# Scaling the exponentials of attention by the head gates, with the first loads in another order

## What is computed

```python
Q, K, V = heads(x @ wq.T + bq), heads(x @ wk.T + bk), heads(x @ wv.T + bv)   # 16 heads of 32
scores = jnp.einsum('bhqd,bhkd->bhqk', Q, K) / sqrt(32)
scores = jnp.where(causal, scores, -1e9)
xm = x.mean(axis=1)                                   # one row per batch
policy_w = softmax(gelu(xm @ sw1.T + sb1) @ sw2.T + sb2)
gates = softmax(einsum(gelu(einsum(xm, pw1) + pb1), pw2) + pb2)
head_gates = jnp.einsum('bp,bph->bh', policy_w, gates)
attn = softmax(scores * head_gates[:, :, None, None])
out = (attn @ V) @ wo.T + bo
```

## Time and profile before

| what | us |
|---|---|
| median of three runs | 1853.58 |
| lowest and highest | 1853.34, 1856.14 |
| the profiled execution, first to last instruction (span) | 1854.0 |
| busy in the span: TensorE | 1693.4 (91%) |
| VectorE | 1387.5 (75%) |
| ScalarE | 1049.5 (57%) |
| GpSimd | 1042.0 (56%) |

### The profile page before, as it was taken

How to read it: one execution, slowest core, us unless ns; L and a number is a source line. 1 busy time by engine, 2 the same in 40 slices (tenths; PEclk the granted TensorE clock), 3 DMA queues, 4 the chain that set the end, 5 groups by cost and what they waited for, 6 DMA issues and landing times. The chain is left out here.

```text
span 1854.0 us, 37186 instructions
## 1 busy us (share of the span) xinstructions
PE 1693.4 (91%) x13426; PEld 763.6 (41%) x13426; DVE 1387.5 (75%) x3039; ACT 1049.5 (57%) x1861; POOL 1042.0 (56%) x1001
## 2 busy tenths in 40 slices
PE   5998999999999999998787999999999998899996
PEld 2433344433433344333233455545455554444432
DVE  7687756777577856688744878878778777788798
ACT  5346555665556655566642556565465454555577
POOL 4049867677775976869872654555555555000044
PEclk9999999999999999999898999999999999899999
DMA  8302112231012311222224223232232131651265
GB/s 274 116 18 61 53 31 58 68 92 42 24 53 78 103 31 25 84 60 81 80 80 164 64 84 101 93 98 97 86 96 88 60 107 47 236 203 46 81 261 187
DMA packets 123039, 172.02 MB, mean 93 GB/s; under 512 B 22376, under 2 KB 73064, under 8 KB 121960
## 3 DMA queue, kind: packets, MB, share of 16 engines
q1 hardware_dynamic: 117336, 160.91, 27.0%
q10 hardware_dynamic: 5520, 8.73, 1.5%
HBM read 106.12 MB, written 38.14 MB: 78 GB/s over the span
## 5 line engine op out<-in xcount | busy, mean ns | idle before, releaser
L1148 DVE CUSTOM_DVE_ANT_0 a_mx<-a_mx,a_mqk 128x128 f32<-128x128 f32 (+3 forms) x512 | 242.0, 511 | 130.7 <-PE a_mx L1348 129.6
L960 ACT ACTIVATE a_P<-a_mx 128x512 f32<-128x512 f32 (+3 forms) x441 | 199.2, 496 | 150.7 <-PE a_mx L1366 80.4
L1231 POOL TENSOR_TENSOR a_P<-a_P 128x512 f32<-128x512 f32 (+3 forms) x202 | 194.2, 990 | 107.7 <-PE a_o L1378 94.6
L1362 PE MATMUL a_mx<-a_Qs,a_Ks 128*128 128x512 f16 (+3 forms) x768 | 231.3, 334 | 19.2 <-ACT a_P L960 7.5
L1348 PE MATMUL a_mx<-a_Ks,a_Qs 96*128 96x512 f16 (+3 forms) x768 | 226.3, 331 | 9.8 <-DVE a_nm L1148 3.0
L960 ACT ACTIVATE share<-a_mx 128x512 f32<-128x512 f32 (+3 forms) x327 | 144.9, 490 | 105.8 <-PE a_mx L1366 59.1
L1231 POOL TENSOR_TENSOR a_P<-a_P,share 128x512 f32<-128x512 f32 (+3 forms) x199 | 184.5, 957 | 27.2 <-ACT share L960 17.4
L1151 DVE TENSOR_REDUCE a_nm<-a_mx 128x1 f32<-128x512 f32 x256 | 164.8, 683 | 31.3 <-PE a_mx L1348 30.4
L2260 PE MATMUL r_pj<-share,cth 128*128 128x512 f16 x672 | 169.6, 386 | 3.6 <-PEq L123 2.7
L2260 PE MATMUL r_pj<-r_xTh,share 128*128 128x512 f16 x512 | 158.9, 383 | 4.4 <-DVE r_xTl L2106 3.7
L3008 PE MATMUL f_pj<-f_xqT,f_wgu 128*128 128x512 bf16 x704 | 158.6, 382 | 0.6 <-DVE f_xqT L2892 0.6
(11 more groups left out here) (302 smaller groups left out, 3999.9 us busy)
## 6 DMA issues: line engine op xcount, KB each, us to landing
x_scratch<-rows SPq DMA_DIRECT2D x60, 256.0 KB, 2.3
rows<-x_scratch SPq DMA_DIRECT2D x56, 256.0 KB, 4.5
lead<-in_xT SPq DMA_DIRECT2D x24, 512.0 KB, 4.4
lead<-in_ctxT SPq DMA_DIRECT2D x38, 256.0 KB, 2.8
h_scratch<-f_h SPq DMA_DIRECT2D x3, 2816.0 KB, 9.1
f_h<-h_scratch SPq DMA_DIRECT2D x3, 2816.0 KB, 9.8
a_Ks<-a_kph SPq DMA_DIRECT2D x256, 32.0 KB, 1.9
a_Qs<-a_qph SPq DMA_DIRECT2D x256, 32.0 KB, 1.9
```

What stands on the lines that cost most here:

```text
L960: act.activation(Pf[pf.at[key]][:, off:512], pb[:, off:512], ACT.Exp).then_inc(p_exp, 1)
L1148: dve.tensor_tensor_reduce(bank_of(it)[:, 0:n], bank_of(it)[:, 0:n], mqk[:, 512 - n:512], 1.0, -3e38, ALU.add, ALU.max, nm[:, col:col + 1] ...
L1231: pool.tensor_tensor(total[:, off:512], total[:, off:512], Pf[pf.at[key]][:, off:512], ALU.add).then_inc(add_pool, 1)
L1362: m = pe.matmul(pb[:, off:512], Ks[s][:, j, kt * P:(kt + 1) * P], Qs[s][:, j, qb * 512 + off:(qb + 1) * 512], start=True, stop=not diag)
```

## The change

1. The Q evictions take a constant scale and the bias `bq` times a constant. They no longer wait for the policy. The exponential takes the gate of its head as its scale, `scale=gates[:, b, h:h + 1]`, a column in SBUF. It waits for the policy's step 9. Step 10 and the mask are gone.
2. The constants and masks are issued by ScalarE, as 14 DMAs ahead of its first split. SyncE loads wk, x, wq, wv, w1. The load of wv now waits for the split of wk, and that of wo for the split of wq.
3. In the plan, K and Q of unit 0 come first, then those of unit 1.
4. The initialisation (`init`, with the casts of the masks) is planned earlier on VectorE, and has a first step for `qbi`.

```diff
         def made():
             done.add(work)
-            put("ACT", work, 1.18, split, lambda: (not u or has(*(("stack", u - 1, n, hf, j) for j in range(4))))
-                and (n == "k" or has(("pol", 1 if b else 0, 10))))
+            put("ACT", work, 1.18, split, lambda: not u or has(*(("stack", u - 1, n, hf, j) for j in range(4))))
...
-            put("ACT", work, 0.08 + 0.00083 * n, out, lambda: room(pf), lambda: pf.take(key))
+            put("ACT", work, 0.08 + 0.00083 * n, out, lambda: room(pf) and has(("pol", 1 if UNITS[u][0] else 0, 9)), lambda: pf.take(key))
...
-        for item, at in ([(("loadw", "wk"), 6.3)] + [(("loadx0", k), 8.0 + k) for k in range(4)]
-                         + [(("loadw1",), 15.5), (("loadw", "wv"), 17.0), (("loadw", "wq"), 20.0), (("consts",), 21.0), (("masks",), 23.0)]):
+        for item, at in ([(("loadw", "wk"), 5.7)] + [(("loadx0", k), 7.8 + 1.2 * k) for k in range(4)]
+                         + [(("loadw", "wq"), 14.0), (("loadw", "wv"), 17.0), (("loadw1",), 22.0)]):
...
-            first = {(0, "k"): -2.0, (1, "k"): -1.8, (0, "q"): -1.8}.get((u, n), u - 2) + QSPAN * i / 4
+            first = (-3.0 if u == 0 else u - 2) + QSPAN * i / 4
...
                 if n == "q":
-                    scale, bias = qsc[:, b, g:g + 1], qbi[:, b, g:g + 1]
-                    w.wait_ge(pol_dve, 24 if b == 0 else 48)
+                    scale, bias = US * HD ** -0.5, qbi[:, g:g + 1]
+                    w.wait_ge(init_dve, 1)
...
                 w.wait_ge(sc_mm, num[it])
+                w.wait_ge(pol_dve, NPOL if b == 0 else 2 * NPOL)
                 p_free(w, key)
-                act.activation(Pf[pf.at[key]][:, off:512], pb[:, off:512], ACT.Exp).then_inc(p_exp, 1)
+                act.activation(Pf[pf.at[key]][:, off:512], pb[:, off:512], ACT.Exp, scale=gates[:, b, h:h + 1]).then_inc(p_exp, 1)
...
-                    dve.tensor_tensor(gsel[:, 0:n, :], bank_of(it)[:, 128:128 + 16 * n].rearrange("p (b h) -> p b h", h=16),
-                                      jmask[:, :].unsqueeze(1).broadcast_to([P, n, 16]), ALU.mult).then_inc(pol_dve, 1)
...
+                    dve.tensor_copy(gates[:, bs, :], bank_of(it)[:, 128:128 + 16 * n].rearrange("p (b h) -> p b h", h=16)
+                                    ).then_inc(pol_dve, 1)
```

More of the change, by code:

```diff
@@ L198 @@
 NP, NPX = 10, 18
-POL = 11
+POL, NPOL = 10, 21
 POLB = [(0, 1), (1, 4)]
@@ L526, in begin @@
     def begin():
-        for item, at in ([(("loadw", "wk"), 6.3)] + [(("loadx0", k), 8.0 + k) for k in range(4)]
-                         + [(("loadw1",), 15.5), (("loadw", "wv"), 17.0), (("loadw", "wq"), 20.0), (("consts",), 21.0), (("masks",), 23.0)]):
+        for item, at in ([(("loadw", "wk"), 5.7)] + [(("loadx0", k), 7.8 + 1.2 * k) for k in range(4)]
+                         + [(("loadw", "wq"), 14.0), (("loadw", "wv"), 17.0), (("loadw1",), 22.0)]):
             flow.order["SP"].append(item)
             after(at, lambda item=item: landed(item))
-        flow.free["SP"] = 19.0
+        flow.order["ACT"].append(("consts",))
+        after(12.0, lambda: put("DVE", ("init",), 1.8, lambda: done.add("init")))
+        flow.free["SP"] = 11.5
         flow.free["POOL"] = 25.0
@@ L539, in lo @@
                 done.add(("w1", name[1]) if name[0] == "w1" else ("splitw", name[0]))
-                if name[0] == "wv":
-                    put("SP", ("loadw", "wo"), 0.5, lambda: after(5.5, lambda: landed(("loadw", "wo"))))
+                if name[0] == "wq":
+                    put("SP", ("loadw", "wo"), 0.5, lambda: after(6.5, lambda: landed(("loadw", "wo"))))
             put("ACT", ("splitw", *name), 1.75, lambda: put("DVE", ("splitw", *name), 2.2, lo))
@@ L680, in attention_phase @@
     hgd = sb("hgd", [4, 4, 16], F32)
-    gsel, gsc = sb("gsel", [P, 4, 16], F32), sb("gsc", [P, 4, 4], F32)
-    qsc, qbi = sb("qsc", [P, 4, 4], F32), sb("qbi", [P, 4, 4], F32)
+    gates, qbi = sb("gates", [P, B, H], F32), sb("qbi", [P, 4], F32)
     bank, obank = ph.banks("mx", 7), ph.banks("o", 1)
@@ L789, in sync @@
                                      ).then_inc(w1_in[i], 16)
[L790 to L800, removed]
             elif kind == "loadx0":
@@ L844, in scalar @@
             kind, key = it[0], it[1:]
-            if kind == "splitw":
+            if kind == "consts":
+                act.dma_start(bqk[:, :], A["bqk"]).then_inc(bqk_in, 16)
+                for i, n in enumerate(("c_ident", "c_mqk", "c_mkq")):
+                    act.dma_start(xtb[i][:, 0:P], A[n]).then_inc(mask_in, 16)
+                for dst, src in ((b1[:, :], A["b1"]), (ones[:, :], A["c_ones"]),
+                                 (sw2[:, :, :], A["sw2T"].rearrange("(k p) c -> p k c", p=P)),
+                                 (pw2[:, :, :], A["pw2T"].rearrange("(k p) c -> p k c", p=P)),
+                                 (b2[:, :], A["b2"][0, :].partition_broadcast(4)), (identf[:, :], A["c_ident"]),
+                                 (cv[:, 0:1], A["clip_x"].partition_broadcast(P)), (cv[:, 1:2], A["clip_down"].partition_broadcast(P)),
+                                 (bvT[:, :], A["bvT"]), (bo[:, :], A["bo"].partition_broadcast(P))):
+                    act.dma_start(dst, src).then_inc(const_in, 16)
+            elif kind == "splitw":
                 n = key[0]
@@ L1058, in vector @@
                     xs = xm[:, bs, :].rearrange("p b k -> p k b")
-                    w.wait_ge(xm_dve, 4 * b1_)
+                    w.wait_ge(xm_dve, max(num[("sumx", b, k)] for b in range(b0, b1_) for k in range(4)))
                     dve.tensor_copy(hi, xs).then_inc(pol_dve, 1)
@@ L3099, in constants @@
         "c_mkq": np.where(n[None, :] < n[:, None], neg, 0.0),
-        "c_jmask": (np.arange(16)[None, :] % 4 == hp[:, None]),
-        "c_cosQ": np.tile(cq, (4, 1)), "c_sinQ": np.tile(sq, (4, 1)),
+                "c_cosQ": np.tile(cq, (4, 1)), "c_sinQ": np.tile(sq, (4, 1)),
         "c_D": dm / (QS * QS),
```

50 lines of the change are left out of this document (20 added, 30 removed).

## The result

| | before | after |
|---|---|---|
| median, us | 1856.58 (19 runs) | 1861.16 (19 runs) |
| lowest and highest | 1853.19, 1861.28 | 1855.32, 1868.38 |
| ratio, with its 95% interval | 1 | 1.0028 (1.0020 to 1.0037) |
| span of the profiled execution | 1854.0 | 1858.9 |

The change makes the kernel 0.28% slower, some 5 us. In what follows a thousandth of the time (a point) is 1.86 us.

The account below looks back on a forecast made before the run. TensorE was taken to bound the long part, other engines counting only where it waits for them. 1854.0 - 8.5 (start) + 18 (column) - 1.5 (Q evictions) = 1862 us; the forecast's own range 1858 to 1870, the whole range 1845 to 1882.

Parts of the forecast that it names:

- a sign of being wrong: Forecast wrong if TensorE's idle time for exponentials stays below 40 us, or the first exponential comes before 90 or after 108.
- The Q evictions' 1.5 us: Q evictions, now with a constant scale, get 5.4 us shorter in all; 1.5 us of it was to reach the total.
- 14 issues at 0.5 us: ScalarE's constant DMAs ahead of its first split: split at 9.0 us instead of 6.43; if four stall, 6 us more.
- First product and first K stack: Start: first product at 19.6 us; first K stack issued at 35.4 instead of 27.7, after 3.8 us waiting for a lead tile.
- First maximum: Start, after SyncE's K and Q stacks: from 73.8 to 56.4 us, with VectorE's list through at 55.5, about the same.
- First exponential: End of the start: 40.3 us of VectorE's steps after the first maximum, so at 96.7 us, 16.7 us earlier.
- The three owed products, 8.2 us: 11 products instead of 14 precede the first score; TensorE owes three at 2.75 us, leaving the start 8.5 us gain.
- The column's 0.085 us in every width: Each of 768 exponentials longer by a fixed 0.085 us: 65 us on ScalarE, 18 of it taken to reach the total.
- the growth of every wait by 0.26 us: TensorE's waits behind bursts of three exponentials each grow by 0.26 us; 53 us if all 208 grew so.
- A: Rival, faster: growth falls in ScalarE's idle time, 5 us reach TensorE, start gives 14: 1845 us; chance 0.27.
- B: Rival: constants land 8 us late, initialisation holds first product and first stack, nothing gained at the start: 1871 us; chance 0.09.
- C: Rival: ScalarE sets the pace in dense stretches and all waits grow, 53 us: 1897 us; chance 0.07.

## Why the prediction came out

The forecast of 1862 us and the sign were right, but two terms were too large with opposite signs. Start and Q evictions were to give 10 us and gave 5.8 (the changed kernel without its column); the column was to cost 18 us and costs 8 to 11. Predicted +8, measured about +5. That the errors cancel is luck. By a sign of being wrong that I named myself, a first exponential after 108 us, the forecast was wrong: it came at 111.1. TensorE's idle time, 40.7 us, just passed the other (below 40). The Q evictions' 1.5 us were not measured apart.

- **14 issues at 0.5 us.** Most took that, but all together 11.8 us, not 7: the tenth stood 3.66 us and the eleventh 0.98. The split of wk came at 13.8 instead of the 9.0 I took, 4.8 late and within the 6 us of my other bound. My reason, nothing large stands ahead on ScalarE's queue, did not hold: among the same first loads the longest constant took SyncE 2.29 us and ScalarE 3.66.
- **First product and first K stack.** Predicted 19.6 and 35.4, measured 25.1 and 40.3. The stack is late by little more than those 4.8 us: the lead tile's wait of 3.8 was 3.45. The first product is another 0.7 late, since the initialisation took 2.5 us and not 1.7.
- **First maximum.** Predicted 56.4, measured 64.4. The first Q stack is at 58.65, so SyncE's order held; the rest is VectorE's, which was still in the policy (64.22) after waits for lead tiles. I had called the two lists about the same.
- **First exponential.** I added what VectorE does from the first maximum on, 40.3 us; it took 46.7. TensorE was the limit there. The windows from 62 us to 113, of the kernel before and then of the changed one, show it:

```profile
62.00:90.00 28.00, 24.75 (x179) 11.80 (x178) 16.60 (x66) 7.66 (x11) 0.00 (x0) 0.88 0.32 87
90.00:113.00 23.00, 20.58 (x96) 8.56 (x95) 20.58 (x62) 5.58 (x9) 0.00 (x0) 1.00 0.12 29
```

```profile
62.00:90.00 28.00, 26.37 (x187) 13.01 (x188) 22.41 (x74) 7.40 (x12) 0.00 (x0) 0.88 0.40 119
90.00:113.00 23.00, 22.34 (x111) 10.08 (x109) 21.87 (x73) 8.70 (x16) 0.00 (x0) 1.00 0.18 46
```

  TensorE is busy 48.7 of 51 us, before 45.3. From the first maximum to the first exponential alone it is busy 46.3 of 46.7 us, VectorE 40.2. This is the step that failed worst: 16.7 us earlier was forecast, 2.3 came. A sum over TensorE would have warned me. From its first product to the first exponential it was busy 84.6 of 98.1 us before; less the three products that is 76.4 us of work, and my forecast left it 77.1 us (19.6 to 96.7). The changed kernel had 74.3 us of work there in 86.0, and no variant had less than 6.5 us of idle time.
- **The three owed products, 8.2 us.** They are owed (132 matmul records of products ahead of the first exponential, before 168), but from first to last exponential the changed kernel without its column takes 845.1 us against 844.3. The debt costs 0.8, not 8.2; TensorE is busy 3.8 us more in that stretch and idle 3 less. So most of the 3.8 was paid out of waits, by these sums and not by a test; why it is 3.8 and not 8.2 is open. So the start's two errors cancel in part as well: 16.7 - 8.2 was forecast, 3.3 - 0.8 is what the two traces show (first exponential 113.4 against 110.1), and 5.8 the ratio of many runs; single executions differ from medians by the rest.
- **The column's 0.085 us in every width.** 0.089 to 0.093. Of the share that reaches TensorE, the idle time for exponentials should rise from 33 to about 50; it rose to 40.7. The step that was mis-sized is the growth of every wait by 0.26 us, 53 us over 208 waits: the weight loads' waits grew by 16 us (kernel before) and 18 (changed). Of this more reached TensorE than the share of 0.28 that I took, 11.0 and 7.6 us. Covered waits did come uncovered, as I had said (44 to 80 and 46 to 70), but they are short ones.
- **Rivals.** A's premise that the growth falls into ScalarE's idle time was mostly right, its start of 14 us was not, though before's order of loads has it. B did not occur in the changed kernel, but at once when the constants were moved. C, where all waits grow, did not occur with one column; with two, the second column's 21 us are still less than half of C's 53. The Trainium skill, "DMA: Bandwidth & Descriptors" (Issuing engines are not separate DMA queues), lets the DMAs of both issuing engines interleave on the same DMA engines, so x should land later. The trace agrees in the direction, with 8.2 us to landing instead of 7.6 in the changed kernel, but it decided nothing, since ScalarE came later still.

What I did not see at all is that the new order of large loads is itself the largest loss at the start: 10 us where SyncE issues the constants (their place in its queue is in that), 11 us where ScalarE does (the initialisation's place is in that). In the change's favour, the order of first products brings 7 us and the gates' leaving the first queries at least as much. Not tried: the column on unit 0 alone, and a start in which wv and w1 keep their order but the lead tiles come earlier.

## What to carry to other kernels

Price an added operand by what reaches the engine that bounds the kernel, not by its duration, and don't take the price of the first for that of the next: the same 69 us cost 8 to 11 us the first time and 21 the second. Before forecasting that a stage gets shorter, add up what the bounding engine has to do in it. Before moving DMA issues to an engine, look at what it waits for first; as many issues as end before that landing are free (seven here), and the later ones delay all behind them. When a change bundles several orders, time each alone: here two parts worth 7 us each hid behind a load order that cost 10 or 11, and the best version (0.9922) takes the former without the latter and pays for the column only in the first batch.

## What was not expected of the hardware

A DMA issue of 0.45 to 0.5 us can stall for several: the tenth of ScalarE's issues took 3.66 us in the changed kernel and 2.81 with before's order of loads. SyncE's issues do it too: in the kernel before, that of wv took 2.63 us at 5.84. Which limit they meet is not shown by these traces.
